# A causal attention's second pass: far tiles ahead of near ones, two heads in one bank, one run of narrow matmuls per step

## What is computed

```python
        H = NUM_HEADS                      # 32
        D = Dm // H                        # 8
        q = _apply_rope(q, cos, sin)
        k = _apply_rope(k, cos, sin)
        scores = jnp.einsum('bhid,bhjd->bhij', q, k) * scale
        diag = i - j
        causal = diag >= 0
        in_band = causal & (diag < MAX_BIAS_LENGTH)      # 128
        bias = jnp.where(in_band, learnable_bias[:, jnp.clip(diag, 0, MAX_BIAS_LENGTH - 1)], 0.0)
        scores = scores + bias[None]
        scores = jnp.where(causal[None, None], scores, -jnp.inf)
        m = jnp.maximum(jnp.max(scores, axis=-1), off)
        p = jnp.exp(scores - m[..., None])
        denom = jnp.sum(p, axis=-1) + jnp.exp(off - m)
        out = jnp.einsum('bhij,bhjd->bhid', p, v) / denom[..., None]
```

## Time and profile before

| | |
|---|---|
| median of 3 runs | 1182.92 us (1181.5 to 1184.55) |
| the profiled execution | 1180.94 us |
| its span in the trace | 1178.8 us |
| PE busy, share of the span | 1008.3 us, 86% |
| DVE busy | 778.1 us, 66% |
| ACT busy | 590.1 us, 50% |
| POOL busy | 402.7 us, 34% |
| first attention's second looks, from the first to the last of them | 181.8 to 501 us of the span |

### The profile page before, as it was taken

How to read it: one execution, slowest core, us unless ns; L and a number is a source line. 1 busy time by engine, 2 the same in 40 slices (tenths; PEclk the granted TensorE clock), 3 DMA queues, 4 the chain that set the end, 5 groups by cost and what they waited for, 6 DMA issues and landing times. The chain is left out here.

```text
span 1178.8 us, 21063 instructions
## 1 busy us (share of the span) xinstructions
PE 1008.3 (86%) x7768; PEld 664.3 (56%) x7768; DVE 778.1 (66%) x1923; ACT 590.1 (50%) x1236; POOL 402.7 (34%) x261
## 2 busy tenths in 40 slices
PE   2899579988888898879989878888898988889697
PEld 1587413333333333368867656666666766667586
DVE  6746996787878776054478646666666666576654
ACT  1643305656665665644256445544545545454264
POOL 4010220314412421000025136554546455555344
PEclk8799858999999988989999999999999999999999
DMA  7020444414432400121010000000000000000001
GB/s 170 1 75 1 145 88 78 83 39 68 91 66 50 78 29 14 52 72 39 34 36 1 1 1 2 1 2 1 2 1 1 1 1 1 2 1 2 1 1 36
DMA packets 25686, 40.26 MB, mean 34 GB/s; under 512 B 3104, under 2 KB 21152, under 8 KB 23808
## 3 DMA queue, kind: packets, MB, share of 16 engines
q1 hardware_dynamic: 25584, 38.93, 14.3%
HBM read 32.88 MB, written 5.84 MB: 33 GB/s over the span
## 5 line engine op out<-in xcount | busy, mean ns | idle before, releaser
L777 POOL TENSOR_SCALAR P<-P,rec 128x1024 f32<-128x1024 f32 (+7 forms) x128 | 220.4, 1724 | 213.3 <-DVE rec L1761 213.3
L901 ACT ACTIVATE PT<-bank 128x512 f32<-128x512 f32 (+3 forms) x384 | 165.8, 492 | 113.1 <-PE bank L1202 95.8
L1632 DVE CUSTOM_DVE_ANT_0 bank<-bank,stripS 128x512 f32<-128x512 f32 (+3 forms) x256 | 148.5, 606 | 49.6 <-PE bank L1177 47.2
L1177 PE MATMUL bank<-KT,QT 96*128 96x512 bf16 (+3 forms) x384 | 127.1, 368 | 35.1 <-DVE MX L1632 23.1
L1391 PE MATMUL bank<-ident,P 128*128 128x128 f32 x576 | 99.0, 281 | 45.9 <-DVE PT L1769 33.6
L1187 PE MATMUL bank<-QT,KT 128*128 128x512 bf16 (+3 forms) x384 | 115.4, 346 | 14.7 <-ACT PT L901 12.8
L1362 PE MATMUL pair<-KH,QH 128*128 128x512 f16 (+3 forms) x576 | 115.0, 327 | 5.6 <-ACT P L967 4.2
L967 ACT ACTIVATE P<-pair,nm 128x1024 f32<-128x1024 f32 (+7 forms) x128 | 95.5, 746 | 43.8 <-DVE nm L1740 43.8
L1403 PE MATMUL bank<-PT,VH 128*128 128x128 f16 x1728 | 117.2, 219 | 0.1
L1403 PEld LDWEIGHTS bank<-PT,VH 128*128 128x128 f16 x1728 | 107.0, 98 | 2.8 <-DVE PT L1769 0.2
L785 ACT ACTIVATE PT<-bank 128x384 f16<-128x384 f32 (+1 forms) x192 | 88.1, 489 | 39.9 <-PE bank L1391 39.1
(11 more groups left out here) (178 smaller groups left out, 1964.9 us busy)
## 6 DMA issues: line engine op xcount, KB each, us to landing
stripS<-band_rows SPq DMA_DIRECT2D x32, 128.0 KB, 2.2
KT<-qk_dram SPq DMA_DIRECT2D x21, 192.0 KB
qk_dram<-parts SPq DMA_DIRECT2D x12, 256.0 KB, 2.2
cprow<-cp SPq DMA_DIRECT2D x9, 256.0 KB, 11.4
stripT<-seq_dram SPq DMA_DIRECT2D x24, 88.0 KB, 9.2
q_raw<-w_gu SPq DMA_DIRECT2D x4, 512.0 KB, 10.7
w_raw<-w_dense SPq DMA_DIRECT2D x2, 1024.0 KB, 6.8
w_raw<-w_q SPq DMA_DIRECT2D x2, 1024.0 KB, 5.5
```

What stands on the lines that cost most here:

```text
L777: pool.tensor_scalar(rows, rows, rec1[:, m % 4:m % 4 + 1], None, ALU.mult).then_inc(s["pn"], 1)
L901: act.activation(PT[:, jb % 2, h, o:o + ni], bank[2 + i2 % 3][:, 0:ni], ACT.Exp).then_inc(s["s2_exp"], 1)
L1177: pe.matmul(ring_bank(use)[:, 0:nj], queries(g)[0:ROWS, h, P * ib:P * (ib + 1)], KT3[0:ROWS, g % 3, h, j0:j0 + nj], start=True, stop=True) ...
L1632: dve.tensor_tensor_reduce(out, out, stripS[:, h, HALF - nj:HALF], 1.0, LOWEST, ALU.add, ALU.max, mx).then_inc(s["s1_max"], 1)
```

## The change

`score_tiles(jb)` replaces `tiles2(jb)` as the list of second-look tiles. It gives the far tile first. A tile whose two heads fit in one bank side by side (width 256 or less) becomes one tile of two heads: two matmuls, one use of a bank, one exponential. So a step has 4 tiles for `jb` 0 and 1, 3 for 2 and 3, 2 for 4 and 5, 1 for 6 and 7; before, it had 4, 4, 4, 4, 2, 2, 2, 2. A group has 40 exponentials, not 48. The order of a step becomes: all its score matmuls with first looks between them, then all its bands and the values without any other matmul between, then what is left of the first looks, and the transposition. The first looks themselves keep their order and their number in each step.

```diff
--- before.py
+++ after.py
@@ -380,7 +380,14 @@
 
             return [(b, max(b * HALF, jb * P), (b + 1) * HALF - max(b * HALF, jb * P)) for b in range(2) if jb * P < (b + 1) * HALF]
 
-        first2 = [sum(GH * len(tiles2(j)) for j in range(jb)) for jb in range(TB + 1)]
+        def score_tiles(jb):
+
+            out = []
+            for b, i0, ni in reversed(tiles2(jb)):
+                out += [(b, i0, ni, (0, 1))] if 2 * ni <= HALF else [(b, i0, ni, (0,)), (b, i0, ni, (1,))]
+            return out
+
+        first2 = [sum(2 * len(score_tiles(j)) for j in range(jb)) for jb in range(TB + 1)]
         N2 = first2[TB]
         LEAD = 12
         PER_STEP = [2, 2, 3, 3, 3, 3, 3, 3, 3, 3, 3, 3, 3, 3, 4, 4]
@@ -404,9 +411,9 @@
 
             return min(2 * P - (i0 - jb * P), ni), i0 - jb * P
 
-        def at_s2(g, jb, h, c):
-
-            return N2 * g + first2[jb] + 2 * len(tiles2(jb)) * (h // 2) + 2 * c + h % 2
+        def at_s2(g, jb, h0, k):
+
+            return N2 * g + first2[jb] + len(score_tiles(jb)) * (h0 // 2) + k
 
         RING = []
         for i in range(GH * N1 + LEAD):
@@ -891,14 +898,14 @@
                 for g in range(NG):
                     for st in range(2 * TB):
                         jb, h0 = st // 2, 2 * (st % 2)
-                        for c, (b, i0, ni) in enumerate(tiles2(jb)):
-                            for h in (h0, h0 + 1):
-                                i2 = at_s2(g, jb, h, c)
-                                act.wait_ge(s["s2"], i2 + 1)
-                                if TB * g + jb >= 2:
-                                    act.wait_ge(s["pv"], TB * g + jb - 1)
-                                o = i0 - jb * P
-                                act.activation(PT[:, jb % 2, h, o:o + ni], bank[2 + i2 % 3][:, 0:ni], ACT.Exp).then_inc(s["s2_exp"], 1)
+                        for k, (b, i0, ni, hs) in enumerate(score_tiles(jb)):
+                            i2 = at_s2(g, jb, h0, k)
+                            act.wait_ge(s["s2"], i2 + 1)
+                            if TB * g + jb >= 2:
+                                act.wait_ge(s["pv"], TB * g + jb - 1)
+                            o = i0 - jb * P
+                            src = bank[2 + i2 % 3][:, 0:len(hs) * ni].rearrange("p (h n) -> p h n", h=len(hs))
+                            act.activation(PT[:, jb % 2, h0 + hs[0]:h0 + hs[-1] + 1, o:o + ni], src, ACT.Exp).then_inc(s["s2_exp"], 1)
                         if st == 0 and g:
                             outputs(g - 1)
                         use = turn(g, st)
@@ -1177,30 +1184,32 @@
                 pe.matmul(ring_bank(use)[:, 0:nj], queries(g)[0:ROWS, h, P * ib:P * (ib + 1)], KT3[0:ROWS, g % 3, h, j0:j0 + nj],
                           start=True, stop=True).then_inc(s["s1"], 1)
 
-            def look2(g, jb, h, c):
-                b, i0, ni = tiles2(jb)[c]
-                i2 = at_s2(g, jb, h, c)
-                if jb == 0 and h % 2 == 0 and c == 0:
-                    pe.wait_ge(m_in[h // 2], 32 * (g + 1))
+            def look2(g, jb, h0, k):
+                b, i0, ni, hs = score_tiles(jb)[k]
+                i2 = at_s2(g, jb, h0, k)
+                if jb == 0 and k == 0:
+                    pe.wait_ge(m_in[h0 // 2], 32 * (g + 1))
                 if i2 >= 3:
                     pe.wait_ge(s["s2_exp"], i2 - 2)
-                ins = pe.matmul(bank[2 + i2 % 3][:, 0:ni], KT3[:, g % 3, h, P * jb:P * (jb + 1)], queries(g)[:, h, i0:i0 + ni],
-                                start=True, stop=True)
+                for j, h in enumerate(hs):
+                    ins = pe.matmul(bank[2 + i2 % 3][:, ni * j:ni * (j + 1)], KT3[:, g % 3, h0 + h, P * jb:P * (jb + 1)],
+                                    queries(g)[:, h0 + h, i0:i0 + ni], start=(j == 0), stop=True, skip_group_check=True)
                 if band_of(i0, ni, jb)[0] <= 0:
                     ins.then_inc(s["s2"], 1)
 
-            def look2_band(g, jb, h, c):
-
-                if jb == 0 and h == 0:
+            def look2_band(g, jb, h0, k):
+
+                if jb == 0 and h0 == 0:
                     pe.wait_ge(strip_t[g % 2], 48 * (g // 2 + 1))
-                b, i0, ni = tiles2(jb)[c]
+                b, i0, ni, hs = score_tiles(jb)[k]
                 n, at = band_of(i0, ni, jb)
                 if n > 0:
-                    for q in range(4):
-                        rows = slice(STRIP_ROWS * q, STRIP_ROWS * (q + 1))
-                        first = STRIP_ROWS * (3 - q) + at
-                        ins = pe.matmul(bank[2 + at_s2(g, jb, h, c) % 3][rows, 0:n], flipb[:, :], stripT[:, g % 2, h, first:first + n],
-                                        start=False, stop=True, skip_group_check=True)
+                    for j, h in enumerate(hs):
+                        for q in range(4):
+                            rows = slice(STRIP_ROWS * q, STRIP_ROWS * (q + 1))
+                            first = STRIP_ROWS * (3 - q) + at
+                            ins = pe.matmul(bank[2 + at_s2(g, jb, h0, k) % 3][rows, ni * j:ni * j + n], flipb[:, :],
+                                            stripT[:, g % 2, h0 + h, first:first + n], start=False, stop=True, skip_group_check=True)
                     ins.then_inc(s["s2"], 1)
 
             def values(g, jb, half):
@@ -1259,22 +1268,18 @@
                     for st in range(2 * TB):
                         jb, h = st // 2, 2 * (st % 2)
                         ahead = look1_at(g, st)
-                        look2(g, jb, h, 0)
-                        look2(g, jb, h + 1, 0)
-                        for i in ahead[:1]:
-                            look1(i)
-                        look2_band(g, jb, h, 0)
-                        look2_band(g, jb, h + 1, 0)
+                        n = len(score_tiles(jb))
+                        for k in range(n):
+                            look2(g, jb, h, k)
+                            for i in ahead[k - 1:k] if k else []:
+                                look1(i)
+                        if n < 2:
+                            for i in ahead[:1]:
+                                look1(i)
+                        for k in range(n):
+                            look2_band(g, jb, h, k)
                         values_at(g, st)
-                        if len(tiles2(jb)) > 1:
-                            look2(g, jb, h, 1)
-                        for i in ahead[1:2]:
-                            look1(i)
-                        if len(tiles2(jb)) > 1:
-                            look2(g, jb, h + 1, 1)
-                            look2_band(g, jb, h, 1)
-                            look2_band(g, jb, h + 1, 1)
-                        for i in ahead[2:]:
+                        for i in ahead[max(1, n - 1):]:
                             look1(i)
                         transposition(turn(g, st))
                 values(NG - 1, TB - 1, 1)
```

## The result

The changed kernel takes 1168.74 us, median of 4 runs (1164.86 to 1170.02), against 1183.74 of the kernel before in the same session (4 runs, 1181.5 to 1186.95): ratio 0.9858, 95% interval 0.9833 to 0.9884. The execution shown is the fastest of the four: its time is 1164.86 us, its span 1162.9.

What follows compares the result with a forecast made beforehand. PE was nearest to full, waiting for DVE and ACT. Gains of 6.5 us in groups 1 to 6 and about 1.0 each in groups 0 and 7 sum to 8.5 us: 1174.4 us forecast, range 1169 to 1181.

Steps and rivals of the forecast that it cites:

- the cover: Step 5's 2.08 us wait for DVE's casts, held by POOL, hides 0.7 us lost in steps 0 to 3.
- The slip of the casts: Rival, chance 0.15: both casts come behind POOL's last instruction, 2.7 us back in all, 1177.1 us.
- the two gains per group: Step 15 into step 0 gains 0.43 us, steps 6 to 8 gain 0.65: 1.08 per group in groups 1 to 6.
- The end of a group: Step 15 into step 0: the 0.65 us wait for ACT goes and a first look comes sooner; gain 0.43 per group.
- Steps 8 to 13: Within steps 8 to 14, which keep PE's order of looks, bands and values: no gain.
- DVE did not eat the gain of steps 6 to 8: Rival, chance 0.12: DVE eats that gain, 0.43 per group stays, with group 7: 1180 us.
- "about 1.0" for group 0: Group 0 loses 0.6 us in its first steps, saves 0.3 in step 5, gains in 6 to 8 and its end.
- Group 7, also "about 1.0": First four steps lose 2.0 us; ACT waits go and merging saves another 1; bounds 2 lost to 3 gained.
- a rival of two stretches of 1.7 us either way: Clock rival, chance 0.15: two more lower-clock stretches cost 3.4 us, giving 1178; two fewer give 1171.
- the rule cited from the Trainium skill: Short idle times between matmul groups over few banks lower the clock; by it this order comes near the slower clock case.
- "Steps 0 to 5": The order loses 0.7 us in steps 0 to 3, hidden in step 5's wait, which becomes some 1.4 us.

Runs made afterwards that it cites:

- the repeated pair: Both kernels unchanged, profiled a second time: the kernel before 1184.04 us, ratio 0.9994; the changed kernel 1169.4 us, 0.9854.
- the look behind: New order, two-head tiles only in steps 6 and 7, third first look of steps 4 and 5 behind bands and values: 1174.76 us, 0.9916.

## Why the prediction came out as it did

**Right: the cover and what it hangs on.** Steps 0 to 3 take 12.00 us (forecast 12.0), the casts end 15.43 after the sum whatever PE does, the wait stays with 1.60 (1.2 to 1.7 named), and moving the sum removes it. The slip of the casts did not come in the changed kernel.

**Right, somewhat small: the two gains per group.** Steps 6 and 7 give 0.71 (0.65 was the term). The end of a group was put at 0.43 and gives 0.51, counted from DVE's first bias and maximum behind the maxima of step 13 to the sum (7.35 before, 6.84 now). Steps 8 to 13 were put at nothing and give 0.14. Together 1.36, by the windows 1.35, against 1.08. DVE did not eat the gain of steps 6 to 8.

**Mis-sized: "about 1.0" for group 0.** It gave 2.7. Its steps 4 to 8 went from 11.09 to 9.80 us, 1.3 by themselves, and 0.5 came in the rest at full clock; the remainder, about 1, is clock (0.91 to 0.95). At full clock it is thus 1.7 or so for the term of 1.0. In the repeated pair the lower clock is on the other side (segment B of group 0 at 1.00 before, at 0.90 changed), and the group gains only 0.9.

**Group 7, also "about 1.0", gave 3.6, and the term was too large.** Steps 0 to 2 would have taken 6.85 before at full clock (10.15 measured, 6.6 of it at half clock, which costs 3.3) and take 8.60 now: 1.7 lost. Step 3 loses another 0.5 (2.49 before, 3.02 now), so the first four steps lose 2.3 where 2.0 had been put. From step 4 on it takes 17.61 instead of 20.23, 2.6 less where 3 had been put (ACT's waits and another 1). That is 0.4 gained, and the clock gave the other 3.3. The waits for ACT in group 7, against the earlier trace rows:

```profile
PE bank L1195 <- ACT PT L908: 1.8, 4, 1.1
PE bank L1225 <- ACT PT L908: 0.5, 2, 0.3
```

**The step that failed: the clock was left at nothing in the sum.** The prediction had it as a rival of two stretches of 1.7 us either way, and found its evidence only in group 7. In the one profile at hand three of the groups 1 to 6 had a granted clock of 0.90 to 0.96 and were longer than the other three. That reading was open to it. The forecast wait was shorter, and with a shorter wait in that place the clock stayed full (next section but one). Between the two traces the orders at full clock give 8.3 us in groups 1 to 6 (6.5 forecast), 1.7 in group 0 and 0.4 in group 7, 10.4 against 8.5; the clock gives 5.3, 1.0 and 3.3, together 9.6 of the 20.0. In the repeated pair the attention is 15.9 us shorter, and the clock is less of it: 4.5 in groups 1 to 6 and 1.8 in group 7 (32.85 us at 0.90 before, 30.71 at 0.94 now), less 0.7 in group 0; that leaves 10.3 for the order, as in the first pair. The 15.0 us of the medians are thus some 10 of order and some 5 of clock. The order by itself, 10.4 for 8.5, would have come out at some 1173 us; the clock carried the time over the edge of the range, narrowly: the second session's median, 1169.4, lies within it. Against the rule cited from the Trainium skill, "TensorE: Matmul & The Clock Gate", section "A second HAM failure mode: psum-queue depth-cycling", this case goes the other way in steps 0 to 8: the short waits for ACT stayed (0.86 and 0.27 above, 1.1 us in all, where the kernel before had 1.1 in four), and the granted clock is 1.00 there in groups 1 to 6 of both profiles.

**Not seen: what the gain depends on.** "Steps 0 to 5" speaks of four tiles and their banks, but not of the place of step 5's third look. With the look in front of bands and values nothing of the gain is left (1.0003).

## To carry to other kernels

Where an engine waits for an event that is fixed elsewhere, put the work that does not depend on it in front of the waiting instruction and let the waiting one come last; a change of order is worth what it moves across that wait. Time lost ahead of such a wait is free until the wait is gone, so look for the wait's own cause first: here moving one DVE sum by four steps gave some 9 us on top of the change, and some 15 with the order in steps 0 to 3 set back. Compare windows at equal granted clock before a difference is put down to instructions, and count lower-clock stretches over more than one profile.

## What the hardware showed beyond what was expected

**In segment A the clock fell behind long waits and not behind shorter ones.** Over all profiles, groups 1 to 6, by the wait at the end of step 5: with a wait of 2.28 us or more the granted clock fell to 1.2 GHz there in 25 of 26 segments (0.87 to 0.93 over the segment); with 2.08 to 2.10, in 7 of 10; with 1.09 to 1.68, in none of 24; with no wait above 1 us there, in none of 18. Two more segments have 0.98, one of the 26 and one of the 18, but theirs is the end of a fall in the segment ahead. The fall begins between 0.7 us before the end of the wait and 1.7 us behind it, and PE then runs at 1.2 GHz (values of 1.92 instead of 1.03 us). This is what was seen, not a threshold: the work on both sides of the wait differs a little between the kernels, and segment B does otherwise.

**Segment B has its own falls, and their cause is open.** In groups 1 to 5 it has no wait above 1.15 us, and the same 1.14 is there, in step 13, in every kernel. Even so its clock is 0.82 to 0.91 in many groups, each time with the fall 0.3 to 1.7 us behind this wait, at a cost of 0.4 to 1.7 us each: in groups 1 to 5 of the changed kernel once in five and four times in five, in all five with the look behind, and in none of the fifteen of the three kernels that have two-head tiles and the old order in steps 0 to 3. Which part of the order does it was not tried.

**A cast of 128x16 can take ten times as long beside POOL.** 0.19 us alone, 0.56 and 2.00 here, with its end within 0.1 us of the end of POOL's instruction of 2.1 us. It was never seen to end in the middle of one. Nor is it the casts alone that are held: in three groups (one of the kernel without two-head tiles in steps 12 to 15, two of the one with the third look ahead) the first cast began as one of POOL's instructions ended and took 0.19 us. The addition behind it, `mt`, then took 2.01 us and ended with POOL's last instruction (321.83 beside 321.79), and the second cast took 0.20. The wait of PE still ended 16.3 us after the sum.
